# Rows turned two tiles ahead, returned rows loaded in halves, and one GpSimd addition in the opening

## The chip, the cores and the metric

The kernel runs on one core of a Trainium2 chip, as one program. Its time is the device time of an execution in microseconds. The core has TensorE (matmuls; PE in the rows, with its weight loads as PEld), VectorE (DVE), ScalarE (ACT), GpSimd (POOL) and SyncE (SP), each with its own instruction queue, in order; they meet only by semaphores, written here as waits for a count. Transfers are started by an engine's queue and run on 16 DMA engines, which all queues share.

## The reference

The input is 8 images of 32 x 32 positions with 128 channels, f32, so 8192 tokens. Four layers follow each other. Each has a mixer over the image and then a feed-forward part with experts (FFN 0 to 3), each added to its input after a normalization:

```python
x = x + conv_i(ln_c(x))        # a box-sum fractal measure, an involution, a spline layer, an attention-like product
t = x as 8192 tokens
t = t + ffn_i(ln_t(t))
```

The FFNs choose experts by a gate, per token:

- FFN 0: 8 experts, one choice, capacity 1.25 x 8192 / 8; relu(x w1 + b1) w2 + b2 with a hidden width of 512; scaled by the probability, NaN and infinities replaced.
- FFN 1: 8 experts, two choices, gelu, hidden width 512.
- FFN 2: 8 experts, two choices, gelu, hidden width 256.
- FFN 3: 16 experts, two choices, silu(x w1) * (x w2), then w3, hidden width 256.

## The kernel before, in words

**How an FFN is laid out.** Every token's row is sent by GpSimd (indirect DMA, L1307) into `dispatched`, a DRAM buffer with one region for each expert. The class `Experts` then works through tiles of 128 rows, all of one expert: T = 72, 136, 136 and 144 tiles in FFN 0 to 3. Results are scattered by GpSimd (indirect DMA, L1756) into `returned`, again in DRAM, in the order of the tokens (one place for each choice). Meanwhile the next layer's first stage (`NormStage`, after FFN 0, 1 and 2; `LastStage` after FFN 3, which the change doesn't touch) loads `returned` image by image (L449), adds it to the residual on VectorE and normalizes it, as a part of the same loop over tiles.

**One tile on the engines.** Tile t has a place t mod 16 in a ring of row buffers `rt` (RING = 16).

- SyncE: `load(t)` (L1490) loads the 64 KB of rows, once the result of tile t - 16 has been scattered (`s_out`). After it, `NormStage.sync_step` issues the load of an image at certain t. In the tiles after the first 32, row loads alternate with the pads of the experts' regions (L972).
- TensorE, step t: `turn_rows(t + 1)` (L1528) transposes the row tile into one of two PSUM banks; `result(t - 2)` (L1546) is the second matmul of an earlier tile; `hidden(t)` (L1536) is the first matmul of this one, on the turned rows `xt` and the expert's weights `wc`, both copied into SBUF with two places each.
- VectorE, step t: in FFN 1 and 2 (`vector_copies`) `copy_weights(t + 1)` (L1652), in all `copy_rows(t + 1)` (L1658, from PSUM to `xt`), in FFN 3 `gate(t)` (L1664), then `scale(t - 2)` (L1674, L1677) of the result, in FFN 0 every second step `guard` (L1687 to L1695), and then what `following` (the next stage) has at this step.
- ScalarE: in FFN 0 and 3 the weight copies (L1589), and the activations (L1599, L1606).
- GpSimd, step t: the scatter of tile t, and what `following` has; early on also the sends of the last images' rows.

TensorE, VectorE and GpSimd run the tiles 16 to 47 in a loop of 16 tiles, with counts from registers; the others are written out.

**What orders the next stage.** The table `STEPS` (L393 to L406) names the step at which SyncE loads image b (`load`), GpSimd folds its two choices into one (`fold`, L469, only in the stage that runs beside FFN 1) and VectorE adds it to the residual (`add`; L487 after a fold, L496 without). `load` counts SyncE's row loads and so runs up to 16 tiles ahead of TensorE. There are two or three rooms for images; `NormStage.load` waits for `rows_added` when it takes a room again. The last two images are loaded after the last tiles (`sync_ahead`, `sync`). An image is 512 KB in the stage beside FFN 0 (one choice) and 1 MB in the other two (two choices).

**The opening** (L174 and on) sets constants and makes the identity and the index tables on GpSimd (L218 to L235), before the first layer.

Of the kernel before, what the change touches and what calls it, by code (L numbers as in the profile page):

```python
# [173 lines left out]
def opening(k):  # L174
# [7 lines left out]
    with ExitStack() as ctx, nc.Block() as block:  # L182
# [38 lines left out]
        def _(pool):  # L221
# [13 lines left out]
            pool.iota(k.token_id1[:], pattern=[[P, NT]], base=0, channel_multiplier=1)  # L235

# [143 lines left out]
class NormStage:  # L380
# [14 lines left out]
        dict(load=(55, 56, 60, 64, 68, 71), add=(46, 48, 52, 56, 60, 66), collect=(48, 50, 54, 58, 64, 68),  # L395
             finish=(60, 70), root=(61, 71), offset=(62, 72), norm=(63, 65, 67, 69, 73, 75),
             turn=(65, 67, 69, 71, 75, 77), keep=(66, 68, 70, 72, 76, 78)),
        dict(load=(87, 88, 89, 93, 103, 119), fold=(75, 77, 79, 83, 91, 108), add=(80, 84, 88, 92, 105, 113),
# [4 lines left out]
        dict(load=(87, 88, 89, 97, 103, 119), add=(90, 93, 96, 99, 107, 120), collect=(94, 97, 100, 103, 111, 124),  # L403
# [4 lines left out]
    def __init__(self, k, layer, spline=None, involution=None):  # L408
# [14 lines left out]
        elif layer == 2:  # L423
            rooms = [k.wts[:, 8192:8192 + 2 * IMG], rows1[:, late:late + 2 * IMG], rows0[:, 3840:3840 + 2 * IMG]]
            slots = [rows0[:, 5888:5888 + IMG], rows0[:, 5888 + IMG:5888 + 2 * IMG], k.ch[:, N:N + IMG]]
        else:
            rooms = [k.wts[:, 7168:7168 + 2 * IMG], rows1[:, late:late + 2 * IMG], rows1[:, 6240:6240 + 2 * IMG]]
            slots = [rows0[:, b * IMG:(b + 1) * IMG] for b in range(B)]
# [15 lines left out]
    def load(self, sp, b):  # L444

        n = len(self.rooms)
        if b >= n:
            sp.wait_ge(*self.when("rows_added", self.adds * (b - n + 1)))
        sp.dma_start(self.room(b), self.src[:, b * TPB:(b + 1) * TPB, :]).then_inc(self.s_back[b].h, 16)  # L449

    def sync_step(self, sp, t):
        for b in range(B - 2):
            if t == self.steps["load"][b]:
                self.load(sp, b)

    def sync_ahead(self, sp, experts):
        experts.results_home(sp, self.COMPLETE[self.layer])
        self.load(sp, B - 2)

    def sync(self, sp):  # L460
        self.load(sp, B - 1)

    def gpsimd_step(self, pool, t):

        for b in range(B - 2):
            if self.folds and t == self.steps["fold"][b]:
                pool.wait_ge(self.s_back[b].h, self.s_back[b].base + 16)
# [21 lines left out]
    def add_half(self, dve, b, c, h):  # L489

        if c == 0:
            dve.wait_ge(self.s_back[b].h, self.s_back[b].base + 16)
# [6 lines left out]
    def add_late(self, dve, b):  # L499

        xs = self.image(b)
        for c in range(self.choices):
# [4 lines left out]
            if c == 0:  # L507
                dve.wait_ge(self.s_back[b].h, self.s_back[b].base + 16)
# [224 lines left out]
    def done(self):  # L733
# [5 lines left out]
        for b in range(B):  # L739
            self.s_back[b].base += 16  # L740
# [651 lines left out]
class Experts:  # L1392
# [5 lines left out]
    def __init__(self, k, layer, ctx, route, following, load_next=None, work_room=None, bias_room=None,  # L1398
# [33 lines left out]
        self.xt, self.wc, self.hs = room(0, 2, C), room(0, 2, wide), room(0, self.HB, F)  # L1432
# [89 lines left out]
    def tensor(self, pe):  # L1522
        k, f, route, s_row = self.k, self.f, self.route, self.s_row

        def turn_rows(t, u):
            pe.wait_ge(s_row[u].h, s_row[u].base + (t - u) * (16 // RING) + 16)

            pe.transpose(k.ps[:, self.PSX + u % 2, 0:P], self.rt[:, u, 0:C], k.ident[:]).then_inc(self.s["x_turned"].h, 1)  # L1528

        def hidden(t, u):  # L1530
            pe.wait_ge(*self.when("x_copied", t + 1))
            if not self.vector_copies:
                pe.wait_ge(*self.when("w_copied", t + 1))

            for j in range(self.wide // P):
                ins = pe.matmul(k.ps[:, self.PSH + u % 2, j * P:(j + 1) * P], self.wc[:, u % 2, j * P:(j + 1) * P],  # L1536
                                self.xt[:, u % 2, :], start=True, stop=True)
# [15 lines left out]
        def step(t, u, last):  # L1553
            at = t if isinstance(t, int) else -1
            if not last:
# [1361 lines left out]
```

## Time and profile before

| | |
|---|---|
| three runs | 2162.23, 2163.42 (median), 2166.87 us |
| the profiled execution | 2167.0 us, span 2165.2 us |
| TensorE busy | 1762.2 us (81%), its weight loads 1383.6 us |
| VectorE busy | 1550.7 us (72%) |
| ScalarE busy | 1200.6 us (55%) |
| GpSimd busy | 957.5 us (44%) |
| DMA | 154.30 MB, mean 71 GB/s |
| tiles of FFN 0, 1, 2, 3 (about) | 361 to 545, 875 to 1163, 1354 to 1592, 1899 to 2149 us |

Shares are of the whole span, and the limit changes from stage to stage. "Idle before" is the time for which an engine did nothing ahead of an instruction, with what ended it; "issue" there means that the profile shows nothing that it waited for. In a timeline a row with xN stands for N instructions one behind the other.

### The profile page before, as it was taken

The numbers are of one execution on the slowest core, as the hardware profiler recorded it, in microseconds if no ns is written. First come the engines' busy times: TensorE is split into PE (matmuls) and PEld (weight loads), VectorE is DVE, ScalarE is ACT, GpSimd is POOL, SyncE is SP. The second block draws the span as 40 slices with busy tenths as digits, with TensorE's granted clock in tenths as the row PEclk, the third lists the DMA queues.
The fourth block names the chain that finished last, engine by engine and source line by source line (L and its number), as shares of the span: only waits on it lengthen the run. The fifth ranks groups of instructions, "written<-read, shape, count | busy, mean of one in ns | idle before, by whom it ended". The sixth has DMA issues, their size and how long they took to land. (4 is left out here: it accounts for less than half of the span.)

```text
span 2165.2 us, 44747 instructions
## 1 busy us (share of the span) xinstructions
PE 1762.2 (81%) x10980; PEld 1383.6 (64%) x10981; DVE 1550.7 (72%) x4814; ACT 1200.6 (55%) x2719; POOL 957.5 (44%) x959
## 2 busy tenths in 40 slices
PE   2687666898588888899896776788859999979996
PEld 2233666897343434799895444667647777778996
DVE  8998887679677777655787576645866677665575
ACT  5455776798333323677685333556655444455664
POOL 0000234444105243675652277777630354557765
PEclk9999666999699999999998787798979999999998
DMA  3002002232201020132531112235422010124365
GB/s 81 0 0 78 18 24 61 60 94 84 87 5 36 22 61 29 56 97 77 151 102 50 56 51 80 70 99 155 138 77 98 20 37 31 54 54 105 100 196 157
DMA packets 183595, 154.30 MB, mean 71 GB/s; under 512 B 40294, under 2 KB 162822, under 8 KB 183362
## 3 DMA queue, kind: packets, MB, share of 16 engines
q1 hardware_dynamic: 153410, 92.37, 16.1%
q0 software_dynamic: 29952, 59.26, 8.1%
q8 instruction: 94, 1.54, 0.3%
q14 instruction: 139, 1.14, 0.2%
HBM read 85.33 MB, written 68.79 MB: 71 GB/s over the span
## 5 line engine op out<-in xcount | busy, mean ns | idle before, releaser
L1756 POOL DMA_INDIRECT returned<-rows_second_choice x488 | 495.9, 1016 | 310.2 <-DVE rows_second_choice L1677 107.4
L1307 POOL DMA_INDIRECT dispatched<-rows_first_choice,slot x192 | 191.9, 999 | 493.7 <-DVE rows_second_choice L1203 441.6
L1536 PE MATMUL psum<-rows_first_choice 128*128 128x128 f32 x2816 | 382.7, 280 | 19.4 <-DVE rows_first_choice L1658 19.2
L1536 PEld LDWEIGHTS psum<-rows_first_choice 128*128 128x128 f32 x2816 | 349.5, 195 | 24.5 <-DVE rows_first_choice L1658 23.5
L1546 PE MATMUL psum<-expert_weights,rows_first_choice 128*128 x2240 | 323.9, 283 | 24.6 <-DVE rows_second_choice L1674 11.0
L1546 PEld LDWEIGHTS psum<-expert_weights,rows_first_choice 128*128 128x128 f32 x2240 | 282.8, 195 | 37.5 <-issue 33.1
L1606 ACT ACTIVATE rows_first_choice<-psum,bias_columns 128x128 f32<-128x128 f32 x832 | 238.4, 375 | 91.3 <-PE psum L1536 89.2
L1307 POOL DMA_INDIRECT dispatched<-rows_second_choice,slot x192 | 187.9, 979 | 58.5 <-issue 58.2
L1307 POOL DMA_INDIRECT dispatched<-rows_first_choice,expert_weights x64 | 61.8, 966 | 266.7 <-DVE rows_first_choice L1201 249.4
L1589 ACT ACTIVATE rows_first_choice<-expert_weights 128x512 f32 x216 | 136.8, 634 | 44.0 <-issue 43.6
L1528 PE MATMUL psum<-identity,rows_second_choice 128*128 128x128 f32 x488 | 137.6, 283 | 14.1 <-DMA rows_second_choice<-dispatched 14.0
L2851 PE MATMUL psum<-channel_major 128*128 128x512 f32 x256 | 131.8, 598 | 1.2 <-ACT channel_major L2769 1.2
L1606 ACT ACTIVATE expert_weights<-psum,bias_columns 128x128 f32<-128x128 f32 x272 | 85.1, 365 | 85.9 <-PE psum L1536 80.7
L1664 DVE TENSOR_TENSOR rows_first_choice<-rows_first_choice,psum 128x256 f32<-128x256 f32 x144 | 60.7, 421 | 87.0 <-ACT rows_first_choice L1599 83.7
L2785 ACT ACTIVATE att_work<-psum 128x512 f32<-128x512 f32 x128 | 73.0, 595 | 90.0 <-PE psum L2851 87.6
L1546 PE MATMUL psum<-expert_weights 128*128 x544 | 101.8, 314 | 24.7 <-DVE rows_second_choice L1677 10.5
L2860 PEld LDWEIGHTS psum<-rows_second_choice,rows_first_choice 128*128 128x128 f32 x680 | 88.7, 192 | 48.6 <-issue 34.6
L1677 DVE SCALAR_TENSOR_TENSOR rows_second_choice<-psum,rows_second_choice,rows_first_choice 128x128 f32<-128x128 f32 x208 | 72.1, 347 | 51.5 <-PE psum L1546 49.8
L1658 DVE COPY rows_first_choice<-psum 128x128 f32<-128x128 f32 x352 | 99.3, 282 | 11.5 <-PE psum L1528 11.0
L1546 PEld LDWEIGHTS psum<-expert_weights 128*128 128x128 f32 x544 | 78.8, 208 | 44.2 <-issue 42.2
L1652 DVE COPY rows_first_choice<-expert_weights 128x512 f32 x136 | 69.0, 507 | 49.9 <-PE psum L1536 45.0
L1536 PE MATMUL psum<-expert_weights 128*128 128x128 f32 x544 | 93.2, 298 | 8.0 <-DVE expert_weights L1658 7.7
(423 smaller groups left out, 3834.1 us busy)
## 6 DMA issues: line engine op xcount, KB each, us to landing
rows_second_choice<-dispatched SPq DMA_DIRECT2D x488, 65.0 KB
rows_second_choice<-returned SPq DMA_DIRECT2D x10, 1024.0 KB, 6.0
returned<-rows_second_choice POOLq DMA_INDIRECT x488
expert_weights<-in_L_ffn_w SPq DMA_DIRECT2D x3, 2048.0 KB, 8.3
expert_weights<-returned SPq DMA_DIRECT2D x6, 1024.0 KB, 5.6
channel_major<-returned SPq DMA_DIRECT2D x6, 1024.0 KB, 7.1
residual<-in_x SPq DMA_DIRECT2D x8, 512.0 KB, 7.3
rows_second_choice<-returned SPq DMA_DIRECT2D x8, 512.0 KB, 4.4
```

Source lines behind the costliest of these rows:

```text
L1307: pool.indirect_dma_start(out=self.k.dispatched, out_offset=bass.IndirectOffsetOnAxis(ap=self.slot[:, b % 2, c, t:t + 1], axis=0), in_=sel ...
L1528: pe.transpose(k.ps[:, self.PSX + u % 2, 0:P], self.rt[:, u, 0:C], k.ident[:]).then_inc(self.s["x_turned"].h, 1)
L1536: ins = pe.matmul(k.ps[:, self.PSH + u % 2, j * P:(j + 1) * P], self.wc[:, u % 2, j * P:(j + 1) * P], self.xt[:, u % 2, :], start=True, st ...
L1546: ins = pe.matmul(self.result_bank(u), self.gs[:, u % self.HB, j * P:(j + 1) * P], self.second[:, bass.ds(e, 1), j, :].rearrange("p a c -> ...
L1589: act.activation(self.wc[:, u % 2, :], self.first[:, bass.ds(e, 1), :].rearrange("p a f -> p (a f)"), ACT.Copy).then_inc(self.s["w_copied" ...
L1606: ins = act.activation(self.hs[:, u % self.HB, cols], k.ps[:, self.PSH + u % 2, cols], f["act"], bias=self.bcol[:, bass.ds(e * self.J + j, ...
L1658: dve.tensor_copy(self.xt[:, u % 2, :], k.ps[:, self.PSX + u % 2, 0:P]).then_inc(self.s["x_copied"].h, 1)
L1677: ins = dve.scalar_tensor_tensor(out=self.ys[:, u, :], in0=self.result_bank(u), scalar=weight, in1=self.wb[:, u % 4, :], op0=ALU.mult, op1 ...
L1756: pool.indirect_dma_start(out=k.returned[0:N * self.K, :], out_offset=bass.IndirectOffsetOnAxis(ap=self.rt[:, u, C:C + 1].bitcast(I32), ax ...
L2785: act.activation(rel[:, g % 3, :], k.ps[:, g % 4, :], ACT.Relu).then_inc(s["att_relu"].h, 1)
L2851: pe.matmul(k.ps[:, g % 4, :], xft[:, b * IMG + j * P:b * IMG + (j + 1) * P], xft[:, b * IMG + h * BANK:b * IMG + (h + 1) * BANK], start=T ...
L2860: ins = pe.matmul(k.ps[:, 4 + h, t * P:(t + 1) * P], r2[g % 3][:, t * P:(t + 1) * P], val[:, b, j * P:(j + 1) * P], start=(j == 0 and t == ...
```

## The change

1. `xt` has four places instead of two. TensorE's step t turns the rows of tile t + 2 instead of t + 1, VectorE's step t copies them; tiles 0 and 1 are turned and copied before the loop. A turn waits until the copy out of its PSUM bank, two tiles before, has been made; a copy waits for the hidden matmul of four tiles before; the hidden matmul waits for the weight copy in all layers. The stage beside FFN 1 has its rooms and slots in `rows0` moved by 256 columns, since the work room is larger.
2. Each returned image is loaded in two halves, with 1, 2 and 2 steps between them in the three stages; who waits for an image waits for both. Some of the steps of loads and folds are new.
3. In the opening GpSimd adds zeros to zeros, 128 x 32, after its index tables, into a small buffer that is not read before it is written again.

```diff
@@ -233,6 +233,8 @@
+            pool.wait_ge(s_set.h, 7)
+            pool.tensor_tensor(k.norm_tmp[:], k.zeros[:, 0:4 * TPB], k.zeros[:, 0:4 * TPB], ALU.add)
...
@@ -392,15 +394,15 @@
-        dict(load=(55, 56, 60, 64, 68, 71), add=(46, 48, 52, 56, 60, 66), collect=(48, 50, 54, 58, 64, 68),
+        dict(apart=1, load=(55, 57, 60, 64, 68, 70), add=(46, 48, 52, 56, 60, 66), collect=(48, 50, 54, 58, 64, 68),
-        dict(load=(87, 88, 89, 93, 103, 119), fold=(75, 77, 79, 83, 91, 108), add=(80, 84, 88, 92, 105, 113),
+        dict(apart=2, load=(87, 90, 93, 96, 103, 119), fold=(75, 78, 81, 85, 92, 108), add=(80, 84, 88, 92, 105, 113),
-        dict(load=(87, 88, 89, 97, 103, 119), add=(90, 93, 96, 99, 107, 120), collect=(94, 97, 100, 103, 111, 124),
+        dict(apart=2, load=(87, 91, 95, 99, 103, 119), add=(90, 93, 96, 99, 107, 120), collect=(94, 97, 100, 103, 111, 124),
...
@@ -421,8 +423,8 @@
-            rooms = [k.wts[:, 8192:8192 + 2 * IMG], rows1[:, late:late + 2 * IMG], rows0[:, 3840:3840 + 2 * IMG]]
-            slots = [rows0[:, 5888:5888 + IMG], rows0[:, 5888 + IMG:5888 + 2 * IMG], k.ch[:, N:N + IMG]]
+            rooms = [k.wts[:, 8192:8192 + 2 * IMG], rows1[:, late:late + 2 * IMG], rows0[:, 4096:4096 + 2 * IMG]]
+            slots = [rows0[:, 6144:6144 + IMG], rows0[:, 6144 + IMG:6144 + 2 * IMG], k.ch[:, N:N + IMG]]
...
@@ -441,30 +443,33 @@
     def slot(self, b, j):
-    def load(self, sp, b):
-        n = len(self.rooms)
-        if b >= n:
+    def load(self, sp, b, h):
+        n, tiles = len(self.rooms), slice(b * TPB + h * TPB // 2, b * TPB + (h + 1) * TPB // 2)
+        if b >= n and h == 0:
-        sp.dma_start(self.room(b), self.src[:, b * TPB:(b + 1) * TPB, :]).then_inc(self.s_back[b].h, 16)
+        sp.dma_start(self.room(b)[:, self.half(h)], self.src[:, tiles, :]).then_inc(self.s_back[b].h, 16)
     def sync_step(self, sp, t):
-            if t == self.steps["load"][b]:
-                self.load(sp, b)
+            for h in range(2):
+                if t == self.steps["load"][b] + h * self.steps["apart"]:
+                    self.load(sp, b, h)
     def sync_ahead(self, sp, experts):
-        self.load(sp, B - 2)
+        for h in range(2):
+            self.load(sp, B - 2, h)
     def sync(self, sp):
-        self.load(sp, B - 1)
+        for h in range(2):
+            self.load(sp, B - 1, h)
     def gpsimd_step(self, pool, t):
-                pool.wait_ge(self.s_back[b].h, self.s_back[b].base + 16)
+                pool.wait_ge(self.s_back[b].h, self.s_back[b].base + 32)
...
@@ -489,7 +494,7 @@
     def add_half(self, dve, b, c, h):
-            dve.wait_ge(self.s_back[b].h, self.s_back[b].base + 16)
+            dve.wait_ge(self.s_back[b].h, self.s_back[b].base + 32)
...
@@ -505,7 +510,7 @@
-                dve.wait_ge(self.s_back[b].h, self.s_back[b].base + 16)
+                dve.wait_ge(self.s_back[b].h, self.s_back[b].base + 32)
...
@@ -737,7 +742,7 @@
-            self.s_back[b].base += 16
+            self.s_back[b].base += 32
...
@@ -1429,7 +1434,7 @@
-        self.xt, self.wc, self.hs = room(0, 2, C), room(0, 2, wide), room(0, self.HB, F)
+        self.xt, self.wc, self.hs = room(0, 4, C), room(0, 2, wide), room(0, self.HB, F)
...
@@ -1524,17 +1529,18 @@
         def turn_rows(t, u):
+            if past(t, 2):
+                pe.wait_ge(*self.when("x_copied", t - 1))
         def hidden(t, u):
-            if not self.vector_copies:
-                pe.wait_ge(*self.when("w_copied", t + 1))
+            pe.wait_ge(*self.when("w_copied", t + 1))
-                                self.xt[:, u % 2, :], start=True, stop=True)
+                                self.xt[:, u % 4, :], start=True, stop=True)
...
@@ -1552,8 +1558,8 @@
         def step(t, u, last):
-            if not last:
-                turn_rows(t + 1, (u + 1) % RING)
+            if not isinstance(t, int) or t + 2 < self.T:
+                turn_rows(t + 2, (u + 2) % RING)
...
@@ -1574,6 +1580,7 @@
+        turn_rows(1, 1)
...
@@ -1649,13 +1656,14 @@
-            dve.tensor_copy(self.wc[:, u % 2, :], self.first[:, bass.ds(e, 1), :].rearrange("p a f -> p (a f)"))
+            dve.tensor_copy(self.wc[:, u % 2, :],
+                            self.first[:, bass.ds(e, 1), :].rearrange("p a f -> p (a f)")).then_inc(self.s["w_copied"].h, 1)
         def copy_rows(t, u):
-            if past(t, 2) and not self.vector_copies:
-                dve.wait_ge(*self.when("hidden_ready", t - 1))
-            dve.tensor_copy(self.xt[:, u % 2, :], k.ps[:, self.PSX + u % 2, 0:P]).then_inc(self.s["x_copied"].h, 1)
+            if past(t, 4):
+                dve.wait_ge(*self.when("hidden_ready", t - 3))
+            dve.tensor_copy(self.xt[:, u % 4, :], k.ps[:, self.PSX + u % 2, 0:P]).then_inc(self.s["x_copied"].h, 1)
...
@@ -1701,8 +1709,8 @@
-            if not last:
-                copy_rows(t + 1, (u + 1) % RING)
+            if not isinstance(t, int) or t + 2 < self.T:
+                copy_rows(t + 2, (u + 2) % RING)
...
@@ -1732,6 +1740,7 @@
+        copy_rows(1, 1)
...
@@ -1763,7 +1772,7 @@
     def done(self):
-        k.advance(x_turned=T, x_copied=T, w_copied=0 if self.vector_copies else T, hidden_ready=T, act_ready=T,
+        k.advance(x_turned=T, x_copied=T, w_copied=T, hidden_ready=T, act_ready=T,
```

## Rows read from the trace of the kernel before

**Rows 1.** The page's part 5: busy, mean ns, and the idle time before, with its releaser.
```profile
L1536 PE MATMUL psum<-rows_first_choice 128*128 128x128 f32 x2816 | 382.7, 280 | 19.4 <-DVE rows_first_choice L1658 19.2
...
L1536 PE MATMUL psum<-expert_weights 128*128 128x128 f32 x544 | 93.2, 298 | 8.0 <-DVE expert_weights L1658 7.7
...
L1528 PE MATMUL psum<-identity,rows_second_choice 128*128 128x128 f32 x488 | 137.6, 283 | 14.1 <-DMA rows_second_choice<-dispatched 14.0
```

**Rows 2.** Windows: stretch, length, busy us (count) per engine, PE clock, DMA share, GB/s.
```profile
430.00:480.00 50.00, 50.00 (x435) 49.90 (x435) 38.28 (x137) 46.48 (x148) 23.58 (x24) 0.97 0.34 93
482.00:520.00 38.00, 32.36 (x271) 30.90 (x272) 37.04 (x140) 31.83 (x97) 17.72 (x17) 1.00 0.38 109
...
1410.00:1490.00 80.00, 68.60 (x491) 59.64 (x492) 44.24 (x163) 49.61 (x164) 61.11 (x63) 0.94 0.39 104
...
1517.00:1555.00 38.00, 28.95 (x176) 22.50 (x177) 34.86 (x138) 19.23 (x64) 23.00 (x19) 0.96 0.56 164
...
2085.00:2148.00 63.00, 61.00 (x499) 57.30 (x497) 50.68 (x145) 37.73 (x77) 42.58 (x39) 1.00 0.73 218
```

**Rows 3.** Timeline, TensorE, FFN 0: start, us, what, [idle before <- releaser].
```profile
427.50 0.45 PE L1528 MATMUL psum<-identity,rows_second_choice 128*128 128x128 f32 x1 [3.92 <-DMA rows_second_choice<-dispatched]
```

**Rows 4.** Waits of TensorE between 482 and 520 us: total, times, longest.
```profile
PE psum L1536 <- DVE rows_first_choice L1658: 6.1, 8, 1.8
```

**Rows 5.** Timeline, SyncE and VectorE, first returned image of FFN 0.
```profile
473.68 0.43 SPq L449 DMA_DIRECT2D rows_second_choice<-returned  x1
...
478.26 0.69 DVE L496 TENSOR_TENSOR residual<-residual,rows_second_choice 128x512 f32<-128x512 f32 x1 [1.58 <-DMA rows_second_choice<-returned]
```

**Rows 6.** Timeline, GpSimd, up to the first fold in FFN 1.
```profile
1027.27 0.98 POOL L1756 DMA_INDIRECT returned<-rows_second_choice  x1 [0.91 <-DVE rows_second_choice L1677]
1029.17 0.98 POOL L1756 DMA_INDIRECT returned<-rows_second_choice  x1 [0.91 <-DVE rows_second_choice L1677]
...
1042.44 2.33 POOL L469 TENSOR_TENSOR expert_weights<-expert_weights 128x1024 f32<-128x1024 f32 x1 [8.50 <-issue]
```

**Rows 7.** Timeline, SyncE, VectorE, TensorE, the same stretch.
```profile
1029.68 0.35 SPq L1490 DMA_DIRECT2D rows_second_choice<-dispatched  x1
...
1035.73 0.33 SPq L1490 DMA_DIRECT2D rows_second_choice<-dispatched  x1
...
1044.80 0.69 DVE L487 TENSOR_TENSOR residual<-residual,expert_weights 128x512 f32<-128x512 f32 x1 [6.43 <-POOL expert_weights L469]
...
1046.08 2.08 PE L1536 MATMUL psum<-rows_first_choice 128*128 128x128 f32 x8 [4.31 <-DVE rows_first_choice L1658]
```

**Rows 8.** Timeline, SyncE, two loads of returned rows in FFN 2.
```profile
1491.49 0.43 SPq L449 DMA_DIRECT2D expert_weights<-returned  x1
...
1516.15 0.39 SPq L449 DMA_DIRECT2D expert_weights<-returned  x1
```

**Rows 9.** Timeline, TensorE, turns of rows in FFN 2.
```profile
1494.69 0.27 PE L1528 MATMUL psum<-identity,rows_second_choice 128*128 128x128 f32 x1
...
1509.24 0.42 PE L1528 MATMUL psum<-identity,rows_second_choice 128*128 128x128 f32 x1
...
1522.03 0.44 PE L1528 MATMUL psum<-identity,rows_second_choice 128*128 128x128 f32 x1 [1.92 <-DMA rows_second_choice<-dispatched]
```

**Rows 10.** Timeline, TensorE, turns of rows in FFN 3.
```profile
2087.78 0.27 PE L1528 MATMUL psum<-identity,rows_second_choice 128*128 128x128 f32 x1
...
2089.23 0.27 PE L1528 MATMUL psum<-identity,rows_second_choice 128*128 128x128 f32 x1
...
2090.93 0.27 PE L1528 MATMUL psum<-identity,rows_second_choice 128*128 128x128 f32 x1
```

**Rows 11.** The page's part 2: GpSimd's busy tenths in 40 slices of the span.
```profile
POOL 0000234444105243675652277777630354557765
```

**Rows 12.** The page's part 6: KB each, median us from issue to landing.
```profile
rows_second_choice<-returned SPq DMA_DIRECT2D x10, 1024.0 KB, 6.0
...
rows_second_choice<-returned SPq DMA_DIRECT2D x8, 512.0 KB, 4.4
```

## The prediction, made before the change was run

> **What bounds the kernel now.** I read the page's list of costly groups first. Of the groups that the diff edits it shows two idle times of TensorE: the hidden matmuls L1536 waited 19.2 us (wide experts) and 7.7 us (FFN 2) for the row copy L1658, and the turns L1528 waited 14.0 us for the DMA of a row tile [rows 1]. These 40.9 us are all that the new places and the second turn could win, if no other engine stood behind the waits. So I read the busy time by stage next [rows 2]. From 430 to 480 us (FFN 0) TensorE is busy for all of 50.00 us: nothing can be won there. From 482 to 520 us VectorE is busy 37.04 of 38.00 us; from 1410 to 1490 us (FFN 2) GpSimd's scatters set the pace, 63 in 80 us or 1.27 us a tile; from 1517 to 1555 us VectorE again, 34.86 of 38.00; from 2085 to 2148 us (FFN 3) TensorE, 61.00 of 63.00. Then the timelines around the single stalls: a late row in FFN 0 [rows 3], the copies' waits and the first returned image there [rows 4, 5], the first fold of FFN 1 [rows 6, 7], the returned loads and late rows of FFN 2 [rows 8, 9], the uneven steps of FFN 3 [rows 10].
>
> **The change part by part.** The profiled run took 2167.0 us (span 2165.2, so 1.8 lie outside it), 3.6 above the median of 2163.42. The terms below are differences, and I put their sum on the median.
>
> *The second turn ahead, FFN 0.* The turn at 427.50 waits 3.92 us for a row that comes when the sends of the last image are over [rows 3]; other work before that row is not moved by the change. Asked for one tile earlier, the wait stands before one more tile of matmuls. A tile is 17 matmuls, and at 435 in 50.00 us [rows 2] that is 1.95 us: +1.9, less what TensorE catches up later. Bounds 0 and +1.9. It could be caught up between 482 and 520, where TensorE waits 6.1 us for copies [rows 4]; but VectorE has 0.96 us idle there, so most of the 6.1 us only changes its name. I take back 1.0. The returned image 0, loaded at 473.68, already keeps the add of VectorE 1.58 us waiting [rows 5]; its second half now leaves one SyncE step later, which the 1.95 us of a tile bound from above and 0 from below; +0.9. FFN 0: +1.8, between -1 and +3.
>
> *FFN 1.* Here the weight copy, not the row copy, is the last thing that a hidden group needs, and it keeps its two places: the row copy's head start saves at most its own place in VectorE's queue. The stage's large stall is the first fold: GpSimd starts the addition at 1042.44 after 8.50 us idle [rows 6], VectorE's add waits 6.43 us for it, and TensorE 4.31 us for the copies queued behind that add, coming back with 2.08 us for 8 matmuls [rows 7], where 435 in 50.00 us make 0.92. The change asks for the first fold at the same step, and I leave this stall as it is. For the next three folds it asks for the second half of an image only after the result two tiles (for the third of them three) before the fold has landed. That chain is: scatter start to the next row issue 2.41 us (1027.27 to 1029.68 [rows 6, 7]), 0.4 for that issue, 4.4 for 512 KB [rows 12], 2.33 for the fold [rows 6], some 9.6 us. The adds that need the folds stand four tiles apart, 4 x 1.95 = 7.8 us. Each turn of the chain is 1.8 us late, three make 5.4; the tile and a half of work that TensorE has queued hides some 1.5 once, and the waits that the old order has at these places go, which I put at 1.9, one tile. FFN 1: +2. Below, if the halves land while the scatters queue anyway: -1. Above: the same distance under load was 1029.17 to 1035.73, 6.56 us [rows 6, 7]; the chain is then 13.7 us, 5.9 late each time, +14 after the same deductions.
>
> *The halves, FFN 2.* Three loads of 1 MB start at 1491.49 and in the next two steps [rows 8]. The turns then go from 1494.69 to 1509.24 in four steps, 3.64 us each, by late rows [rows 9]. The new order spreads the same bytes over eight steps. The step is then between GpSimd's 1.27 us and the 1.94 us of 1517 to 1555 (176 matmuls, 9 a tile, in 38.00 us) [rows 2]; I take 1.6, the middle. Four steps save 4 x (3.64 - 1.6) = 8.1 us, with bounds 6.8 and 9.5. The load of image 3 waits at SyncE until image 0 has been added, and leaves at 1516.15 [rows 8]; behind it the rows wait, and the turn at 1522.03 comes 1.92 us late [rows 9]. Image 0 is added some 8 us sooner, so I take this as gone too: -10.0. Against it: the adds follow at steps 93, 96 and 99, but the second halves leave at SyncE's steps 93, 97 and 101. VectorE would wait in front of its copies if SyncE were fewer than about three steps ahead (4.4 us at 1.6), and from 1517 it is full in any case, so I expect none of the 7.7 us of waits for copies [rows 1] back there. I give back 2. FFN 2: -8, between -3 (three adds late by half a landing, 2.2 us, each) and -11 (9.5 and 1.9).
>
> *FFN 3.* Steps alternate there, 1.45 us (2087.78 to 2089.23) and 1.70 (to 2090.93) [rows 10], since VectorE's copy came just late; with a copy one tile ahead all could take 1.45. The 499 matmuls, 13 a tile, are 38 tiles; at a mean saving of 0.125 they would give 4.8 us. VectorE is busy 50.68 of 63.00 [rows 2] and part of the late copies come from its adds, so I take 3.9. Where SyncE alternates row loads with pads, rows come later than TensorE wants them, and each is now wanted one step earlier: once a step of 1.45, +1.5. FFN 3: -2.4, between -4.8 and +1.5.
>
> *What is left.* The last two images of each of three stages are two issues instead of one, 0.43 us each [rows 5]; mostly beside the landing of the first half: +0.4. The new waits of TensorE on copies already done cost nothing where TensorE has work queued: FFN 0, which has the wait for the weight copy already, runs without a gap [rows 2]. Two more turns before the loop stand beside the first row's landing. The opening's addition is 128x32; the fold is 32 times that and takes 2.33 us [rows 6], and GpSimd is idle for most of the first four slices of the span [rows 11]: 0, bounded above by the fold's 8.50 us were it on the path, and below by rival A.
>
> Sum: +1.8 + 2 - 8 - 2.4 + 0.4 = -6.2 us; 2163.4 - 6.2 = 2157.2, about 2157 us.
>
> **The rivals.** *A, the opening's addition spares the first fold's stall.* The gap of 8.50 us before the fold is put down to nothing but issue [rows 6], while the load of its image left ahead of the row load of 1029.68 [rows 7], 12.8 us sooner, and 1024 KB land in 6.0 [rows 12]. If it is the price of the first addition on GpSimd, the opening pays it now, and of the stall TensorE's 4.31 us and the 1.16 us of its slow matmuls go: 5.5 us more, 2152. For it: the gap comes once. Against it: between the opening and FFN 1 GpSimd runs other kinds of operation (scatters, a reduction over partitions), which may drive the addition's code out again. The Trainium skill ("GPSIMD Engine Reference", 2.1 Instruction dispatch) says that the first call into a freshly loaded kernel pays some 6 us for loading its code. The size agrees with the 8.50 us; whether the load comes once or again after another library the trace of before doesn't show.
>
> *B, FFN 2 gives little.* If VectorE, full from 1517 us, only starts its queue sooner and then waits for second halves, 3 us of the 8 remain: 2162, no change. For it: 34.86 of 38.00 [rows 2]. Against it: before 1517 the rows, not VectorE, end the waits [rows 9].
>
> *C, slower: the fold chain in FFN 1.* At the loaded distance of 6.56 us, FFN 1 costs +14 instead of +2, and the sum is +6, 2169; it turns the sum from a chain of 13.1 us on (three times 5.3 late, less 3.4, is 12.5 instead of 2). Halves also carry fewer bytes a microsecond: 4.4 us for 512 KB against 6.0 for 1024 [rows 12], so two in turn take 8.8. The Trainium skill ("DMA: Bandwidth & Descriptors", Bandwidth) advises batches of 1 MiB or more, and the trace agrees as far as these two medians go. Against C: the large loads themselves are what made that distance 6.56, and halves two steps apart load the DMA engines less.
>
> *D, the change doesn't do what it says:* the row copies' waits become weight copies' waits everywhere, and rows turned earlier only wait earlier. Then FFN 3 gives 0 and the sum is about -2.3: 2161.
>
> **How the numbers follow.** A difference under 0.2% (4.3 us) can't be told from none here. Chances: forecast 0.42, A 0.25, B with D 0.18, C 0.15. Faster than 2159.1: two thirds of the forecast's cases, nearly all of A's, a few of B's, 0.28 + 0.24 + 0.03 + 0.03 (C, if FFN 2 gives 11 beside it) = 0.58. Slower than 2167.7: 0.11 of C, 0.03 of the forecast, 0.02 of B and D = 0.16. Between: 0.26. The range runs from A with the best of FFN 2 and FFN 3 (2152 - 3 - 2.4, and 1 for FFN 0: 2146) to C's 2169; I leave some 0.07 below it and 0.11 above.
>
> **What would show it.** Right: in FFN 2 the four turns from step 86 take under 8 us and no row is late near 1520; in FFN 3 the steps after 2086 are 1.45; the row at 427 is still late, one tile sooner; folds 1 to 3 wait for their DMA. The first fold's gap tells A. Wrong: waits of VectorE's adds in FFN 2 for second halves (B), waits of GpSimd of over 5 us before folds 1 to 3 with TensorE behind (C), weight copies (L1652, and L1589 of ScalarE in FFN 3) in place of L1658 as TensorE's releaser at the same length (D).

## The result, and the profile after

The changed kernel is slower. Its median is 2174.73 us (six runs, 2171.84 to 2177.21) against 2164.14 us for the kernel before (six runs); the ratio is 1.0044, with a 95% interval of 1.0032 to 1.0057. Forecast was 2157 us, range 2146 to 2169. The profiled execution has a span of 2173.1 us, 7.9 more than before. (The profiled execution of the kernel before, 2167.0 us, lies 2.9 above the median of its six runs; so the traces place 7.9 of the 10.6 us.)

**Where the 7.9 us arose.** To follow the loss I compare when TensorE starts a step: the turn rows of the two traces, where the changed kernel's step t holds the turn of one tile later. The lag against the kernel before, in us, from step 2 to the last turn of each stage, and at some places between:

| stage | lag at its start | on the way | lag at its end | the stage's own | predicted |
|---|---|---|---|---|---|
| FFN 0 | -0.6 | 0.8 (step 48), 4.6 (step 50) | 6.3 | +6.9 | +1.8 |
| FFN 1 | 5.4 | 2.5 (step 90), 8.1 (step 103) | 8.0 | +2.6 | +2 |
| FFN 2 | 8.4 | 10.2 (step 40), 16.6 (step 86), 5.4 (step 100) | 5.3 | -3.1 | -8 |
| FFN 3 | 5.5 | 8.9 (step 45), 7.1 (step 107) | 7.5 | +2.0 | -2.4 |

What lies outside these stretches adds -0.5 us in all. These are single profiles: a stretch with the same edits can differ by 2 to 3 us between two of them (steps 2 to 40 of FFN 1: +0.2 here, +2.8 in e3 below, which has the same code there), so a stage's figure is good to about that.

The page's groups that answer to [rows 1], part 5 of the changed kernel (L1542 is the hidden matmul, L1535 the turn, L1659 the weight copy on VectorE, L1552 the result):

```profile
L1542 PE MATMUL psum<-rows_first_choice 128*128 128x128 f32 x2816 | 379.2, 278 | 10.0 <-DVE rows_first_choice L1659 10.0
...
L1535 PE MATMUL psum<-identity,rows_second_choice 128*128 128x128 f32 x488 | 136.5, 281 | 18.4 <-DMA rows_second_choice<-dispatched 9.2
...
L1552 PEld LDWEIGHTS psum<-expert_weights 128*128 128x128 f32 x544 | 76.1, 202 | 58.2 <-issue 57.8
```

and TensorE's waits over the whole span (total, times, longest):

```profile
PE psum L1542 <- DVE rows_first_choice L1659: 10.0, 6, 2.9
...
PE psum L1535 <- DMA rows_second_choice<-dispatched: 9.2, 5, 5.7
PE psum L1535 <- DVE rows_first_choice L1666: 7.7, 7, 3.1
```

The waits for the row copy in front of the hidden matmul, 19.2 us before, are gone from the list by name. Half of them came back as waits for the weight copy, and the turn, which never waited for a copy before, now waits 7.7 us for the copy that frees its PSUM bank (L1666). A wait that disappears from a page has not been saved until the step that it stood in is shorter.

**FFN 0.** The late row of [rows 3] is met one tile sooner, as foreseen, and leaves 1.2 us of lag (from step 21 to step 25). The next large loss is image 0. SyncE's and VectorE's rows that answer to [rows 5]:

```profile
473.48 0.33 SPq L1495 DMA_DIRECT2D rows_second_choice<-dispatched  x1
473.86 0.43 SPq L451 DMA_DIRECT2D rows_second_choice<-returned  x1
477.25 0.34 SPq L1495 DMA_DIRECT2D rows_second_choice<-dispatched  x1
477.63 0.43 SPq L451 DMA_DIRECT2D rows_second_choice<-returned  x1
```
```profile
483.18 0.69 DVE L501 TENSOR_TENSOR residual<-residual,rows_second_choice 128x512 f32<-128x512 f32 x1 [5.67 <-DMA rows_second_choice<-returned]
```

The first half leaves as early as the whole image did. The second half stands in SyncE's queue behind the next row load, and that one waits for a scatter until 477.25, 3.77 us after the row load before it. VectorE's add, 1.58 us late before, is 5.67 us late now, and the lag of TensorE grows by 3.7 us within two steps. This profile is the worst of four: in e2, e3 and e4, which have the same loads beside FFN 0, the second half leaves 2.28, 3.77 and 2.38 us after the first, the add waits 2.98, 3.92 and 2.60 us, and the lag grows by 1.4, 1.4 and 0.1 us in these two steps.

**FFN 1.** GpSimd's folds in the changed kernel, for [rows 6]:

```profile
1046.76 2.33 POOL L474 TENSOR_TENSOR expert_weights<-expert_weights 128x1024 f32<-128x1024 f32 x1 [7.24 <-issue]
...
1056.83 2.35 POOL L474 TENSOR_TENSOR rows_second_choice<-rows_second_choice 128x1024 f32<-128x1024 f32 x1 [2.88 <-DMA rows_second_choice<-returned]
...
1067.19 2.35 POOL L474 TENSOR_TENSOR rows_first_choice<-rows_first_choice 128x1024 f32<-128x1024 f32 x1 [3.76 <-DMA rows_first_choice<-returned]
...
1077.53 2.34 POOL L474 TENSOR_TENSOR expert_weights<-expert_weights 128x1024 f32<-128x1024 f32 x1 [2.47 <-DMA expert_weights<-returned]
```

The first fold's stall is still there, 7.24 us, and each of the next three waits for its second half; they start 10.1 to 10.4 us apart. The chain was worked out at 9.6.

**FFN 2.** The turns that answer to [rows 9]:

```profile
1511.32 0.27 PE L1535 MATMUL psum<-identity,rows_second_choice 128*128 128x128 f32 x1
...
1512.75 0.27 PE L1535 MATMUL psum<-identity,rows_second_choice 128*128 128x128 f32 x1
...
1514.18 0.27 PE L1535 MATMUL psum<-identity,rows_second_choice 128*128 128x128 f32 x1
...
1515.50 0.27 PE L1535 MATMUL psum<-identity,rows_second_choice 128*128 128x128 f32 x1
...
1516.83 0.27 PE L1535 MATMUL psum<-identity,rows_second_choice 128*128 128x128 f32 x1
```

Steps 86 to 90 take 5.51 us instead of 14.55, and no row is late near step 97: 12.3 us of lag vanish between steps 86 and 98. Part of the 14.55 us was clock: in the kernel before, TensorE's granted clock is 0.62 on average from 1494 to 1512 us, between full speed (2.4 GHz) and half of it (1.2 GHz), after waits for rows of up to 2.00 us, and [rows 9] show a turn of 0.42 us there against 0.27. In the changed kernel it is 1.00 from 1495 to 1517. Nor are the 12.3 us all won by the halves, as e1 shows below.

But 6.4 us had been lost between steps 40 and 86. There TensorE's step went from 1.20 us (1494.69 - 1439.28 over 46 steps) to 1.34 (1511.32 - 1449.50). How one such step looks, first before, then after:

```profile
1452.97 0.27 PE L1528 MATMUL psum<-identity,rows_second_choice 128*128 128x128 f32 x1
1453.09 0.71 PE L1546 MATMUL psum<-expert_weights 128*128 x4
1453.63 0.61 PE L1536 MATMUL psum<-expert_weights 128*128 128x128 f32 x4
1454.08 0.27 PE L1528 MATMUL psum<-identity,rows_second_choice 128*128 128x128 f32 x1
```
```profile
1466.32 0.27 PE L1535 MATMUL psum<-identity,rows_second_choice 128*128 128x128 f32 x1
1466.73 0.71 PE L1552 MATMUL psum<-expert_weights 128*128 x4
1467.28 0.61 PE L1542 MATMUL psum<-expert_weights 128*128 128x128 f32 x4
1467.72 0.27 PE L1535 MATMUL psum<-identity,rows_second_choice 128*128 128x128 f32 x1
```

The reader is to look at the distance from the turn to the result behind it: 0.12 us before, 0.41 after; everything else in the step is as long as it was. The granted clock is 1.00 in both stretches, so it is not the clock. The idle time is put down to nothing but "issue" (ahead of the result's weight loads, 14.4 us in 46 places between 1449 and 1511, against 5.8 in 16 places in the same steps before).

### The profile page after: what moved, and what is told of

The parts are those of the page before. It is cut to its first block and busy times, and to the rows that moved or that the text cites. A ratio compares the mean times of both kernels' runs of the same rounds, so it can differ in the third digit from the quotient of the medians.

```text
span 2173.1 us, 45671 instructions
## 1 busy us (share of the span) xinstructions
PE 1764.4 (81%) x10964; PEld 1376.6 (63%) x10981; DVE 1544.3 (71%) x4814; ACT 1201.9 (55%) x2719; POOL 959.6 (44%) x960
## 5 line engine op out<-in xcount | busy, mean ns | idle before, releaser
L1542 PE MATMUL psum<-rows_first_choice 128*128 128x128 f32 x2816 | 379.2, 278 | 10.0 <-DVE rows_first_choice L1659 10.0
L1542 PEld LDWEIGHTS psum<-rows_first_choice 128*128 128x128 f32 x2816 | 349.2, 195 | 11.1 <-issue 11.0
L1552 PE MATMUL psum<-expert_weights,rows_first_choice 128*128 x2240 | 324.3, 283 | 36.2 <-DVE rows_second_choice L1682 14.0
L1552 PEld LDWEIGHTS psum<-expert_weights,rows_first_choice 128*128 128x128 f32 x2240 | 281.1, 193 | 54.9 <-issue 49.6
L1535 PE MATMUL psum<-identity,rows_second_choice 128*128 128x128 f32 x488 | 136.5, 281 | 18.4 <-DMA rows_second_choice<-dispatched 9.2
L1552 PE MATMUL psum<-expert_weights 128*128 x544 | 100.7, 310 | 30.2 <-issue 12.1
L1552 PEld LDWEIGHTS psum<-expert_weights 128*128 128x128 f32 x544 | 76.1, 202 | 58.2 <-issue 57.8
L1666 DVE COPY rows_first_choice<-psum 128x128 f32<-128x128 f32 x352 | 98.8, 281 | 14.2 <-PE psum L1535 13.5
L1659 DVE COPY rows_first_choice<-expert_weights 128x512 f32 x136 | 60.1, 442 | 51.3 <-PE psum L1542 45.9
L2869 PE MATMUL psum<-rows_second_choice,rows_first_choice 128*128 128x128 f32 x680 | 90.4, 276 | 6.6 <-DVE rows_first_choice L2828 6.6
```

The costliest lines, as they stand in the source:

```text
L1552: ins = pe.matmul(self.result_bank(u), self.gs[:, u % self.HB, j * P:(j + 1) * P], self.second[:, bass.ds(e, 1), j, :].rearrange("p a c -> ...
L1666: dve.tensor_copy(self.xt[:, u % 4, :], k.ps[:, self.PSX + u % 2, 0:P]).then_inc(self.s["x_copied"].h, 1)
L2869: ins = pe.matmul(k.ps[:, 4 + h, t * P:(t + 1) * P], r2[g % 3][:, t * P:(t + 1) * P], val[:, b, j * P:(j + 1) * P], start=(j == 0 and t == ...
```

## The experiments

The theory after the result: the second turn ahead is the loss, through its two new waits in TensorE's queue and through rows and copies that are met sooner; the halves lose in FFN 0 and 1 what they win in FFN 2; the opening's addition does nothing. Each kernel was timed against the kernel before on the same chip; ratios are against it, with 95% intervals.

| run | median us | ratio | interval |
|---|---|---|---|
| e1, second turn ahead alone | 2176.7 | 1.0057 | 1.0040 to 1.0074 |
| e2, halves and steps alone | 2163.52 | 0.9992 | 0.9983 to 1.0002 |
| e3, changed kernel without the addition | 2173.99 | 1.0040 | 1.0027 to 1.0053 |
| e4, changed kernel, two waits fewer | 2170.07 | 1.0022 | 1.0010 to 1.0034 |
| e5, before, addition behind the reduction | 2159.59 | 0.9975 | 0.9962 to 0.9988 |
| e6, before, halves beside FFN 2, e5's addition | 2150.94 | 0.9940 | 0.9925 to 0.9955 |
| e7, before, whole loads spaced beside FFN 2 | 2159.06 | 0.9972 | 0.9961 to 0.9982 |
| e8, changed kernel, whole loads beside FFN 0 | 2172.26 | 1.0035 | 1.0023 to 1.0047 |
| e9, e6 with the second turn ahead in FFN 3 | 2154.76 | 0.9957 | 0.9944 to 0.9971 |
| e10, before with two more waits | 2164.94 | 1.0001 | 0.9991 to 1.0010 |

### The change taken apart: e1, e2, e3

e1 has the parts of the diff in `Experts` and the moved rooms; e2 those in `STEPS`, `load` and its callers; e3 all but this:

```diff
-            pool.wait_ge(s_set.h, 7)
-            pool.tensor_tensor(k.norm_tmp[:], k.zeros[:, 0:4 * TPB], k.zeros[:, 0:4 * TPB], ALU.add)
```

> The second turn ahead alone (four places, the waits, the moved rooms), with the loads whole and at the old steps and without the addition. Theory: the second turn ahead is what makes the changed kernel slower. In FFN 2 the two added waits make TensorE's short steps longer (1.34 us instead of 1.21 between steps 40 and 86), in FFN 0 and FFN 3 a late row or a busy VectorE is met one tile sooner; 7 to 11 us slower than the kernel before, 2171 to 2175. Rival: the second turn ahead is neutral and the halves are what costs: within 3 us of the kernel before, and the steps of FFN 2 stay at 1.21.

> The halves and the new steps of loads and folds alone, with one turn ahead and without the addition. Theory: FFN 0 loses 3 to 5 us to the later second half of image 0 (VectorE's add waits over 4 us), FFN 1 some 2.5 to the fold chain, FFN 2 gains 8 to 12: 4 to 8 us faster than the kernel before, 2156 to 2160. Rival: twice as many transfers slow the rows in every stage, FFN 2 gives 3 or less, and this kernel is slower than before, 2168 or more.

> The changed kernel without the opening's addition. Theory: the addition changes nothing, since GpSimd's code is changed for the reduction in the first mixer and again at the first fold: within 3 us of the changed kernel (2172 to 2178), the gap before the first fold still 7 to 8.5 us. Rival: the addition does shorten the first fold's gap (7.24 us against 8.50), and without it the gap is 8.5 or more and the kernel 1 to 2 us slower.

e1 is 0.57% slower, 1.7 us beyond the upper number expected; e2 can't be told from no change, where 4 to 8 us were expected; together 0.49%, about the 0.44% of the whole. So the second turn ahead accounts for the whole loss. By stages, from the same turn rows, e1 costs +3.0 (FFN 0), +2.2 (FFN 1), +2.4 (FFN 2) and +3.0 us (FFN 3): it wins nowhere. In its FFN 2 the lag grows by 6.4 us from step 40 to step 86 and falls by 7.8 in the next four steps. These take 6.71 us there, with whole loads at the old steps: the rows for which TensorE waited 4.3 us before are nearly all there (0.6 us) when it asks for them later. So four short steps are no sign of the halves. What the halves give by themselves is read from e2: its lag grows by only 0.7 us from step 40 to step 86, and the four steps take 7.11 us. e2 costs +2.2 in FFN 0 and +5.2 in FFN 1, and wins 9.9 in FFN 2. In FFN 0 less was lost than expected (the add waited 2.98 us, not over 4). The miss of e2's expectation is FFN 1: five kernels have these folds, and the stage cost them +2.6 (the changed kernel), +5.0 (e4), +5.2 (e2), +6.3 (e8) and +6.5 (e3, of which 2.8 lie in steps 2 to 40, before any fold), so the changed kernel's own profile flattered it.

e3 is as slow as the changed kernel. The first fold's gap is 8.41 us there, but 7.11 in e2, which has no addition either, and with it, in the changed kernel, e4 and e8, it is 7.24, 7.90 and 7.09: the length varies by itself. The addition changes nothing where it stands.

### The waits of TensorE: e4, e10

e4 lets one wait stand for three in FFN 1 and 2; e10 puts the two waits into the kernel before, where both are on events long past:

```diff
 def turn_rows(t, u):
-            if past(t, 2):
+            if past(t, 2) and (not self.vector_copies or isinstance(t, int) and t == 2):
 def hidden(t, u):
+            if self.vector_copies and (not isinstance(t, int) or t + 1 < self.T):
+                pe.wait_ge(*self.when("x_copied", t + 2))
+            else:
...
```
```diff
 def turn_rows(t, u):
+            if past(t, 2):
+                pe.wait_ge(*self.when("x_copied", t - 1))
...
 def hidden(t, u):
...
-            if not self.vector_copies:
-                pe.wait_ge(*self.when("w_copied", t + 1))
+            pe.wait_ge(*self.when("w_copied", t + 1))
...
```

> The changed kernel with as many waits of TensorE per tile in FFN 1 and 2 as before: the hidden matmul waits for the row copy of the next tile, which VectorE makes after the weight copy of this one, and so the waits for the weight copy and for the turn's bank go. Theory: the two added waits themselves lengthen FFN 2's short steps; from 40 to 86 they take 1.20 to 1.25 us instead of 1.34, and the kernel is 4 to 7 us faster than the changed kernel, 2168 to 2171. Rival: the steps are longer for another reason (the order of turn and result, or GpSimd's pace): 1.34 as before, and no gain.

> The kernel before with two more waits of TensorE per tile in FFN 1 and 2, on events that are long past (the weight copy, the copy out of the turn's bank); the turn stays one tile ahead. Theory: the waits alone make FFN 2's short steps longer, since nothing hides them behind a single turn: some 1.34 us a step between steps 40 and 86 instead of 1.21, idle time ahead of the result's weight loads 12 us or more instead of 5.8; of it most is given back before step 100 since GpSimd was behind anyway, so the total changes by -1 to +4 us. Rival: waits on past events are free, and it was the order of the turns: 1.21 and no change in any stage.

e4's lag grows by 1.6 us from step 40 to 86 instead of 6.4 (a step of 1.24 us), and it is some 4.7 us faster than the changed kernel (their intervals meet at the edge). e10's lag grows by 7.1 us there (1.36 us a step) with the turn one tile ahead as before. Idle time ahead of the result's weight loads, in e10 from 1439 to 1496, and in e4 from 1449.5 to 1508:

```profile
PEld psum L1547 <- issue: 14.0, 42, 0.6
```
```profile
PEld psum L1555 <- issue: 4.3, 16, 0.8
```

So the waits themselves take the time, not the order of the turns. It isn't the clock, which is granted at 1.00 in e10's stretch too, nor the count that VectorE now raises behind each weight copy, which e4 has as well. In e10 the lag is 7.0 at step 86 and 1.3 at step 100, and the total is that of the kernel before: in the kernel before, the late rows of [rows 9] hold up a TensorE that comes earlier for just as much longer. Where the halves take that hold-up away, as in the changed kernel, the lost time is no longer given back in full; by the stage lags that is the 3.4 us between e2's -8.2 and the changed kernel's -4.8 from step 40 to step 120, and e4's is -7.6.

### Image 0 beside FFN 0: e8

```diff
-        dict(apart=1, load=(55, 57, 60, 64, 68, 70), add=(46, 48, 52, 56, 60, 66), collect=(48, 50, 54, 58, 64, 68),
+        dict(load=(55, 56, 60, 64, 68, 71), add=(46, 48, 52, 56, 60, 66), collect=(48, 50, 54, 58, 64, 68),
...
+        self.parts = 1 if layer == 1 else 2
```

> The changed kernel with whole loads at the old steps beside FFN 0, the rest as changed. Theory: the later second half of image 0 is what VectorE's add waits 5.67 us for, and costs 3 to 4 us; with the whole load the wait is 1.5 to 3 us, FFN 0 ends 2 to 4 us sooner, 2170 to 2173. Rival: the turn two tiles ahead, which waits for VectorE's copies there, is the cause: FFN 0 ends as late as in the changed kernel.

VectorE's first add waits for 1.33 us:

```profile
479.52 0.69 DVE L502 TENSOR_TENSOR residual<-residual,rows_second_choice 128x512 f32<-128x512 f32 x1 [1.33 <-DMA rows_second_choice<-returned]
```

The lag at the end of FFN 0 is 1.5 us instead of 6.3, so the halves there cost 4.8 in these two profiles. The medians differ by 2.5 only, and their intervals overlap; e8 loses more than the changed kernel in FFN 1, as above. Other profiles agree with 2 to 3 us: with the second turn ahead, FFN 0 ends at a lag of 6.3, 6.4 (e3) and 4.7 (e4) with halves and of 3.9 (e1) and 1.5 (e8) with whole loads; with one turn ahead, at 2.6 (e2) with halves and at -0.1 to 1.8 in the five kernels with whole loads.

### Which part of the new loads wins in FFN 2: e7

```diff
-        dict(load=(87, 88, 89, 97, 103, 119), add=(90, 93, 96, 99, 107, 120), collect=(94, 97, 100, 103, 111, 124),
+        dict(load=(87, 91, 95, 99, 103, 119), add=(90, 93, 96, 99, 107, 120), collect=(94, 97, 100, 103, 111, 124),
```

> The kernel before with only the steps of the loads beside FFN 2 changed, to 87, 91, 95, 99, and each image whole. Theory: what the new order gives in FFN 2 is mostly the spacing: three loads of 1 MB no longer meet; 5 to 8 us faster in FFN 2 (2157 to 2161), the halves adding 1 to 3. Rival: one load of 1 MB is enough to hold a row up, so that without halves the late rows stay: 2 us or less.

5.6 us faster by the medians; from step 40 to 120 its lag falls by 6.1 us. With halves it falls by 8.2 (e2) and 7.4 us (e6) there. The spacing is most of the gain.

### Where the addition has to stand: e5

```diff
             pool.partition_all_reduce(rngall[:].rearrange("p a b -> p (a b)"), rng[:].rearrange("p a b -> p (a b)"), P,
                                       bass.bass_isa.ReduceOp.max).then_inc(s["mix_allmax"].h, 1)
+            pool.tensor_tensor(k.norm_tmp[:], k.zeros[:, 0:4 * TPB], k.zeros[:, 0:4 * TPB], ALU.add)
```

> The kernel before with the small addition of GpSimd placed behind the reduction over partitions in the first mixer, instead of in the opening. Theory: the gap before the first fold is a change of GpSimd's code, which the reduction makes necessary; behind it, the addition takes the change at some 56 us, where nobody waits, and the fold of FFN 1 starts when its rows are there (gap under 2 us). TensorE's step excess there goes: 4 to 7 us faster than the kernel before, 2157 to 2161. Rival: scatters and sends drive the code out again, or the gap is something else: gap 7 to 8.5 us as before, no change (within 3 us).

5.1 us faster. GpSimd's rows of e5, first the reduction and the addition, then the first two folds of FFN 1:

```profile
55.78 0.40 POOL L2016 PARTITION_ALL_REDUCE range_all<-range  x1 [52.13 <-DVE range L1906]
62.98 0.55 POOL L2018 TENSOR_TENSOR norm_tmp<-zeros 128x32 f32<-128x32 f32 x1 [6.80 <-issue]
```
```profile
1036.45 2.35 POOL L469 TENSOR_TENSOR expert_weights<-expert_weights 128x1024 f32<-128x1024 f32 x1 [1.72 <-DMA expert_weights<-returned]
...
1041.33 2.39 POOL L469 TENSOR_TENSOR rows_second_choice<-rows_second_choice 128x1024 f32<-128x1024 f32 x1
```

The gap has moved to 56 us, 6.80 long, where nobody waits for GpSimd, and the fold waits 1.72 us for its own data. What stands at the start of the gap is in the traces: two rows by which GpSimd's queue changes the engine's configuration, ahead of the first fold in the kernel before and ahead of the addition in e5, where the fold has none:

```profile
L469 POOLq MODIFY_POOL_CONFIG  x2: 57/57/57, 1034.0 to 1034.0; - x2
```
```profile
L2018 POOLq MODIFY_POOL_CONFIG  x2: 88/88/88, 56.1 to 56.2; - x2
```

All twelve kernels have such rows at 1.9 us, at 37.4 to 38.3 us ahead of the reduction, and at the first addition behind the reduction, and nowhere else. So rival A had the right cause and the wrong moment: the opening pays nothing (the addition took 0.24 us at 3.6 us in the changed kernel), and the reduction behind it makes the change necessary again. Neither the scatters nor the sends of two FFNs undo it.

### What remains when each part stands where it wins: e6, and FFN 3 by itself: e9

e6 is the kernel before with halves and new steps for FFN 2 alone (`self.parts = 2 if layer == 3 else 1`, the load steps of e7 with `apart=2`) and e5's line. e9 adds the second turn in FFN 3:

```diff
+        self.ahead = 2 if layer == 3 else 1
-        self.xt, self.wc, self.hs = room(0, 2, C), room(0, 2, wide), room(0, self.HB, F)
+        self.xt, self.wc, self.hs = room(0, 2 * self.ahead, C), room(0, 2, wide), room(0, self.HB, F)
```

> The kernel before with the halves and new load steps only in the stage beside FFN 2, whole loads and old steps beside FFN 0 and 1, one turn ahead, and the addition behind the reduction. Theory: the stages are separate, so FFN 2 gives the 8 to 9 us that the halves alone gave there, the addition some 5, nothing is lost elsewhere: 2149 to 2154. Rival: the gain in FFN 2 came from FFN 1's later end (other phases of the rows) and is 3 or less: 2157 or more.

> The kernel with the halves beside FFN 2 and the addition behind the reduction (2150.9 us), with the second turn ahead in FFN 3 alone. Theory: there the second turn gives nothing, because the gate on VectorE and not the row copy ends the waits after 2087, and it loses where rows come late between the pads: 1 to 4 us slower than without it, 2151 to 2155. Rival: the losses of FFN 3 in the changed kernel came from its different start, and the stage by itself gains the 2 to 4 us that were predicted: 2147 to 2149.

e6 beats both kernels: 2150.94 us, 0.60% faster than the kernel before. e9 takes 3.8 us of that back by the medians (3.6 by the lag at the end of FFN 3), though the two intervals overlap. The turns of FFN 3 in the changed kernel still alternate, for [rows 10]:

```profile
2094.85 0.27 PE L1535 MATMUL psum<-identity,rows_second_choice 128*128 128x128 f32 x1
2095.26 0.71 PE L1552 MATMUL psum<-expert_weights,rows_first_choice 128*128 x4
...
2096.70 0.27 PE L1535 MATMUL psum<-identity,rows_second_choice 128*128 128x128 f32 x1
2096.82 0.71 PE L1552 MATMUL psum<-expert_weights,rows_first_choice 128*128 x4
...
2098.26 0.27 PE L1535 MATMUL psum<-identity,rows_second_choice 128*128 128x128 f32 x1
```

1.85 and 1.56 us; from step 110 to step 140 a step takes 1.62 us on average, against 1.60 before. In the kernel before, TensorE's waits from 2085 to 2148 us name the row copy once only:

```profile
PE psum L1536 <- DVE rows_first_choice L1658: 1.0, 1, 1.0
```

In the changed kernel the idle time stands ahead of the result (0.41 us behind the turn of 2094.85) and no longer ahead of the hidden matmul. Whether the gate's lateness or the new wait in TensorE's queue is behind it was not tried apart.

## Why the prediction was wrong

The sum was -6.2 us; 10.6 were lost by the medians. By the stages' lags, term by term:

- **FFN 0, +1.8, measured +6.9.** The late row came as said, but the 1.0 us taken back for it after 482 did not come: in e1 and e8, with whole loads, the lag changes by +1.0 and 0.0 us from step 48 to the end. The other step that failed is "its second half now leaves one SyncE step later, which the 1.95 us of a tile bound from above". A step of SyncE is no tile of TensorE: the half stands behind a row load that waits for a scatter, and left 3.77 us after the first half (2.28 to 3.77 in four profiles). The add's wait grew by 4.09 us where +0.9 was taken; over all the profiles the halves cost 2 to 3 us there.
- **FFN 1, +2, measured +2.6, and +5.0 to +6.5 in other kernels with the same folds.** The chain (9.6 us predicted, 10.1 to 10.4 measured) was right. What failed are the deductions of 1.5 and 1.9 us, which left 2 of 5.4: the lag grew by 5.6 us from step 90 to step 103 (4.2 to 8.2 in e2, e3, e4 and e8). That the stage's own figure is lower here comes from the first fold, around which 3.1 us were won (step 80 to step 90).
- **FFN 2, -8, measured -3.1.** The new loads did what was forecast: 9.9 us by themselves (e2), most of it by the spacing (e7), and no wait of VectorE for second halves, so rival B falls, though its number, 3 us left of the 8, came out by another cause. "The four turns from step 86 take under 8 us" was no test of them, since e1 passes it with the old loads. What failed is "The new waits of TensorE on copies already done cost nothing where TensorE has work queued". The row behind it was FFN 0, with 17 matmuls a tile; in FFN 2, with 9, the result followed the turn by 0.12 us, and e10 shows 0.15 us a tile for two waits on past events. That a short step has no room to hide a wait in is my reading of these two cases. Steps 2 to 40 lost 1.8 us more (1.5 to 3.0 in all five kernels with the second turn ahead in FFN 2, e4 among them); what is behind that stays open.
- **FFN 3, -2.4, measured +2.0.** "With a copy one tile ahead all could take 1.45" failed: the steps stayed uneven and as long as before on average, and from step 86 to the end the lag fell by 0.6 us where 3.9 were taken. That the row copy makes them uneven was never in the rows. From step 2 to step 86 2.6 us were lost where +1.5 was taken for late rows, but the rows weren't late: TensorE waited 0.2 us for one from 1905 to 1990 us, while its result's waits for VectorE's scaling (L1674, now L1682) grew from 10.3 to 12.3 us. What is behind both stays open. Rival D was right in kind (FFN 3 gave nothing, and elsewhere L1659 and L1666 took L1658's place), but not in price.
- **Rival A** was given 0.25. The addition as placed spares nothing (e3); moved, it gives 5.1 us (e5), near the 5.5 worked out for it. That the trace of the kernel before couldn't tell whether the load comes again was wrong: its rows of the configuration, at 37.8 us for the reduction and at 1034.0 for the fold, stand between the opening and the first fold. The Trainium skill ("GPSIMD Engine Reference", 2.1 Instruction dispatch) puts the loading of a kernel's code at about 6 us. The gaps are longer here: 6.70 to 7.03 us behind the reduction (e5, e6, e9), 7.09 to 10.22 at the fold in the nine other kernels; why they differ was not tried.
- **Rival C** named a place that lost, but not for its reason: it wanted a chain of 13.1 us or more and waits of over 5 us before the folds, and they were 10.1 to 10.4 and 2.47 to 3.76. It was only one of four places that lost (FFN 0, FFN 1, the short steps of FFN 2, FFN 3). No single rival was the cause; the terms were treated as if the worst of each could not come together. The upper bound of FFN 0 (+3) was passed, and that of FFN 3 (+1.5) too, but by no more than two profiles differ.

## What to carry to other kernels

An added semaphore wait that was free in steps of 17 matmuls was not free in steps of 9: look at the shortest step, not at the fullest stage. Before a transfer is split, look at what stands between its halves in the issuing engine's queue; spacing whole transfers may give most of the gain. Look for GpSimd's configuration rows in the trace: if a change can't be avoided, let a small operation ask for it at a time when nobody waits, after the last operation that makes it necessary. And where one loss can be given back by the next wait, a short stretch proves little: compare kernels that differ in one part.

## What the runs showed of the hardware

- Two waits of TensorE on semaphores that had long reached their counts made a step of 9 matmuls 0.15 us longer (1.20 to 1.36 us, e10), and left FFN 1's steps of 17 matmuls as they were (the lag is 0.60 us at step 40 and at step 80).
- The first addition on GpSimd behind a reduction over partitions stood behind an idle time of 6.70 to 7.03 us when it was asked for at 56 us (e5, e6, e9) and of 7.09 to 10.22 us at the first fold (the nine other kernels), each time behind a change of the engine's configuration; in e5 some 970 us of scatters and sends in between did not bring it back.
- Time that TensorE lost ahead of late rows was given back there: in e10 7.0 us of lag at step 86 were 1.3 at step 100, and the total ratio 1.0001.
